# Edge counts summed two tiles ahead of their mask, and source rows requested before the next residual tile

## What is computed

```
xn = layernorm(x)
attn = numerator / max(denominator, 1e-6)                 # first mixer, 8 heads
x_mid = x + attn @ proj_w.T + proj_b + gat(xn, src, dst)
# gat, for each of 4 heads: h = xn @ W
e = leaky_relu(as_[src] + ad_[dst], 0.2)
m = segment_max(e, dst); e = exp(e - m[dst])
alpha = e / segment_sum(e, dst)[dst]
out = segment_sum(h[src] * alpha, dst)
```

## Time and profile before

| | value |
|---|---|
| median of 3 runs | 2633.81 us |
| range of the runs | 2632.14 to 2635.1 us |
| the profiled execution, its device time | 2630.19 us |
| its span in the trace | 2628.4 us |
| TensorE busy | 2555.2 us, 97% of the span |
| VectorE busy | 1587.2 us, 60% |
| ScalarE busy | 769.6 us, 29% |
| GpSimd busy | 347.7 us, 13% |
| mean DMA rate | 61 GB/s |
| VectorE count sums, L1580 | 10 of 1.45 us |
| VectorE masked maxima, L1613 | 100 of 1.46 us in the program, 40 in this stage |

### The profile page before, as it was taken

The page is one execution under the profiler, slowest core; times in us unless marked ns, Lnnn a source line. Parts: engine busy times, 40 slices in busy tenths (PEclk is TensorE's granted clock), DMA queues, the critical chain, the costliest instruction groups (busy, mean ns, idle before and its releaser), DMA issues.

```text
span 2628.4 us, 26650 instructions
## 1 busy us (share of the span) xinstructions
PE 2555.2 (97%) x10594; PEld 1813.6 (69%) x10594; DVE 1587.2 (60%) x2708; ACT 769.6 (29%) x1291; POOL 347.7 (13%) x197
## 2 busy tenths in 40 slices
PE   7999999999999997999999999999999999999999
PEld 4667667558965996777777775565755786556676
DVE  4456471779948996987888998254342561341322
ACT  1043342006732863222222221430002331332000
POOL 0888888000000000000000000000000000000000
PEclk9999999999999998999999999999999999999999
DMA  9232313543020406000120003200450100213201
GB/s 257 26 44 14 50 2 50 143 145 123 20 80 20 116 1 215 1 0 1 72 102 0 24 24 115 70 1 1 115 164 18 37 1 1 63 37 126 87 24 59
DMA packets 139168, 160.74 MB, mean 61 GB/s; under 512 B 96618, under 2 KB 108484, under 8 KB 137516
## 3 DMA queue, kind: packets, MB, share of 16 engines
q1 hardware_dynamic: 68323, 158.60, 19.4%
q0 software_dynamic: 70720, 0.43, 2.8%
HBM read 122.75 MB, written 35.87 MB: 60 GB/s over the span
## 4 chain that ended last, share of the span: by engine, by line
PE 51%; DVE 7%; ACT 2%; issue 1%; DMA 0%; SPq 0%; DVEq 0%; ACTq 0%
PE psum L521 51%; DVE arena L1863 2%; DVE arena L1865 1%; DVE arena L1864 1%; PE psum L532 0%; DVE arena L1856 0%; ACT arena L1126 0%; ACT arena L1131 0%; ACT arena L1015 0%; DVE arena L1519 0%; DVE arena L1929 0%; DVE arena L1361 0%; DVE arena L1862 0%; DVE arena L1855 0%; DVE arena L1888 0%
## 5 line engine op out<-in xcount | busy, mean ns | idle before, releaser
L521 PE MATMUL psum<-arena 128*125 128x384 f32 (+12 forms) x9762 | 2454.4, 413 | 34.8 <-DMA arena<-in_ffn_w 7.1
L521 PEld LDWEIGHTS psum<-arena 128*125 128x125 f32 (+3 forms) x9762 | 1719.8, 188 | 745.5 <-issue 136.7
L2278 POOL DMA_INDIRECT count_matrix<-arena x170 | 343.0, 2018 | 121.1 <-DVE arena L1458 59.7
L1863 DVE RECIPROCAL arena<-arena 128x500 f32<-128x500 f32 x60 | 196.7, 3278 | 2.1
L1613 DVE CUSTOM_DVE_ANT_0 arena<-arena 125x1250 bf16<-125x1250 bf16 (+1 forms) x100 | 139.2, 1458 | 12.9 <-DMA arena<-source_rows 8.3
L2288 POOL MEMSET arena<- 125x60 f32 x1 | 0.2, 208 | 1039.4 <-PE psum L521 1039.4
L1697 DVE TENSOR_TENSOR arena<-arena 125x1250 f32<-125x1250 f32 x80 | 116.3, 1453 | 13.7 <-ACT arena L1108 13.6
L1105 ACT ACTIVATE arena<-arena 125x1250 f32<-125x1250 f32 x80 | 106.9, 1336 | 56.7 <-PE psum L521 56.5
L1700 DVE SCALAR_TENSOR_TENSOR arena<-arena 125x1250 f32<-125x1250 f32 x80 | 116.9, 1461 | 2.8
L1015 ACT ACTIVATE arena<-psum 128x250 f32<-128x250 f32 (+1 forms) x102 | 40.6, 494 | 231.4 <-PE psum L532 230.9
L1248 ACT ACTIVATE arena<-psum,arena 128x250 f32<-128x250 f32 x120 | 49.3, 465 | 198.6 <-PE psum L521 198.6
(11 more groups left out here) (226 smaller groups left out, 1435.0 us busy)
## 6 DMA issues: line engine op xcount, KB each, us to landing
arena<-in_ffn_w SPq DMA_DIRECT2D x3, 4608.0 KB, 14.9
residual<-arena SPq DMA_DIRECT2D x30, 336.0 KB
arena<-residual SPq DMA_DIRECT2D x30, 336.0 KB
arena<-target_rows SPq DMA_DIRECT2D x12, 610.4 KB
arena<-in_gat_w SPq DMA_DIRECT2D x3, 2304.0 KB, 10.5
arena<-residual SPq DMA_DIRECT2D x10, 672.0 KB
residual<-arena SPq DMA_DIRECT2D x10, 672.0 KB
count_matrix<-arena SPq DMA_DIRECT2D x2, 3125.0 KB, 26.9
```

The source lines that it names most:

```text
L521: return pe.matmul(o, lhsT, rhs, start=start, stop=stop, skip_group_check=share)
L1863: now(dve.reciprocal(t_, t_))
L2278: pool.indirect_dma_start(counts[k], bass.IndirectOffsetOnAxis(ap=IDX_I[0:T, c:c + 1].bitcast(U32), axis=0), COUNT_I[0:T, c:c + 1], None, ...
```

## The change

Three things are altered.

1. DVE sums the counts of tile j + 2 behind the mask of tile j, where it summed those of tile j + 1. To begin, it sums tiles 0 and 1 ahead of the first projection. The number of sums stays ten.
2. SP asks for the counts of tile 5 at t = 1 and no longer at t = 2. The other tiles' counts are asked for where they were.
3. SP issues source rows 0 and 1, with the wait for the last mask ahead of them, behind the store of tile 4 and ahead of the wait for that store and the load of tile 6. They were issued behind the load of tile 6. Source row 2 stays where it was.

```diff
-COUNTS_BESIDE = {0: (3,), 1: (4,), 2: (5, 6), 3: (7, 8), 4: (9,)}
+COUNTS_BESIDE = {0: (3,), 1: (4, 5), 2: (6,), 3: (7, 8), 4: (9,)}
...
-                if j + 1 < NT:
-                    count_sum(j + 1)
+                if j + 2 < NT:
+                    count_sum(j + 2)
...
             count_sum(0)
             source_scores(0)
+            count_sum(1)
...
-                if t == 6:
+                if t == 9:
+                    source_row(0, 2)
+
+            def behind_projection(t):
+                if t == 4:
                     sp.wait_ge(as_saved, 16)
                     sp.wait_ge(v_drained, V_AT[("mask", NT - 1, 2)] + 1)
                     source_row(0, 0)
                     source_row(0, 1)
-                if t == 9:
-                    source_row(0, 2)
-
-            residual(0, x, SLOT_M, res[XMID0], beside_projection, begun=True)
+
+            residual(0, x, SLOT_M, res[XMID0], beside_projection, behind=behind_projection, begun=True)
```

## The result

The changed kernel takes 2625.81 us, the median of 12 runs (2623.5 to 2630.97). The kernel before, in 12 runs of the same sessions, takes 2632.2 us. The ratio of the two is 0.9979 with a 95% interval of 0.997 to 0.9988: 5.5 us faster, between 3.2 and 7.9 (the plain difference of the two medians is 6.4). In a later session the same pair gave 0.9986 (0.9977 to 0.9995), 3.7 us, with medians only 2.0 apart. So the size of the gain is known to two or three microseconds and no better. I had forecast 5.0 us and a time between 2626.7 and 2632.0. The profiled execution has a span of 2624.1 us, 4.3 less than the 2628.4 of before.

A forecast was written before the change was run, and what follows sets the result against it. TensorE was taken as the bound, with VectorE nearly as loaded and the order of work causing PE's stalls. 3.97 - 0.6 + 1.68 = 5.0 us, taken from 2633.81, gave 2628.8 us, range 2626.7 to 2632.0.

The forecast's parts named there:

- the source rows' head start: Before the first attention: rows issued 2.8 us earlier land 2.75 us earlier, and that gain reaches L1697 in full.
- The sum: Whole kernel: 3.97 from the masks, less 0.6 for late counts, plus 1.68 at the attention, 5.0 us gained.
- 3.97 us for the masks, at most: Mask stage: TensorE no longer waits for count sums before tiles 3, 5, 7 and 9, four times 0.99 us.
- Rival D: Mask stage: PE stops as before, on the ring of banks; gain 1.7 us, time 2632.1, chance 0.04.
- 0.6 us given back by late counts: Mask stage: DVE waits 0.5 to 0.9 us each for counts of tiles 7 and 9; PE loses 0.3 to 1.05.
- My room of 0.75: Mask stage's ring of banks: PE doesn't stop as long as DVE loses less than 0.75 us in all.
- 1.68 us at the attention: First attention matmuls: DVE holds PE from 610.92 to 612.60; earlier source rows remove this 1.68 us.
- Rival C: Source rows: their head start is not passed on; gain 3.4 to 3.9 us, time 2629.9 to 2630.4, chance 0.12.
- What is now behind the rows: DMA queue: tile 6's load, put behind the rows, lands at 545.9, just before DVE wants it at 546.6.
- The stores of the mask: Before the attention: stores of CT and NEG move by as much as the maxima; DVE didn't stand at their wait before.
- The masks' ring: Mask stage: a half's last three of four banks wait for the previous half's mask banks; room 0.75 us.

The follow-up runs named there:

- the execution with early counts: The changed kernel profiled once more without edit; ratio to the kernel before 0.9986, median 2627.45 us.
- its second profile: The kernel before, profiled once more without edit; span 2625.5 us, ratio 1.0007.
- two kernels: Changed kernel with each source row written by two DMAs (0.9974), and changed kernel with unsplit rows requested at t = 5 (0.9977), ratios to the kernel before.
- rows-alone kernel: Against the changed kernel, sums and count loads put back as before, only the source rows issued earlier; ratio to the kernel before 0.9996.
- the sums alone: Against the changed kernel, source rows put back as before, sums two ahead and tile 5's earlier count load kept; ratio to the kernel before 0.999, median 2626.13 us.
- the second pair: The kernel before and the changed kernel, each profiled once more without edit; ratios 1.0007 and 0.9986.
- the kernel with the delay: Changed kernel plus two needless VectorE copies ahead of the first attention weights; ratio to the kernel before 0.9983.
- the swapped order: Changed kernel with each half's projection ahead of its mask on TensorE and VectorE; ratio to the kernel before 0.9973, median 2623.54 us.

## Why the prediction was wrong

Two steps failed. One put the time outside the range (the level), the other is in the mechanism (the source rows' head start).

**The range.** What put the time outside was mostly the level. I took the median of three runs, 2633.81, for the level of the kernel before. Its median of 12 is 2632.2, 1.6 lower, and in three later sessions it is 2629.4 to 2630.9. The forecast gain of 5.0 us under 2632.2 gives 2627.2; the time came 1.4 below that, as the plain difference of the medians is 6.4 and not 5.0; the ratio puts the gain at 3.2 to 7.9, so that part is within the noise. I had read "three runs spread over 3 us" and still allowed only 1 us of scatter above and 1.5 below. This is the step that put the time outside: "The median of runs lies 3.6 above that execution; I take the same distance", with 1.5 us of room downward. Three runs don't fix the level so closely.

**The sum** came near the measured gain, 5.0 against 5.5 and 3.7, but partly by luck. It contains 1.68 us at the attention that the runs don't show as a gain, and it leaves out the clock, whose single fall is worth as much. That the total came out is no evidence for its terms.

*3.97 us for the masks, at most:* right. With the counts early the halves are 4.96 us apart throughout, and the four stalls of the earlier trace rows are gone in every kernel that sums two ahead. Rival D, that the ring stops TensorE anyway, is refuted.

*0.6 us given back by late counts:* right in mechanism, too small. The waits were 1.3 to 1.5 and 0.7 to 0.9 us, where I had 0.5 to 0.9 each (tile 9's fits, tile 7's doesn't). The part mis-sized is the landing: SP's steps were as predicted (store waited for 2.74, load of x 0.8), but tile 7's counts, followed in the queue by those of tile 8, took 5.4 us from first issue to VectorE's start (501.99 to 507.39) and not 4.51. Tile 9's, with nothing behind, took 4.8. My room of 0.75 was for an execution in which VectorE waits for its first counts and TensorE doesn't start late. None of the profiles is of that kind: the room is 1.15 without VectorE's wait, which agrees with 0.75, as the wait was to be 0.4 to 0.6, and 1.83 where TensorE was late too. Loss: 1.3 in the execution with early counts, 0.2 in the one whose clock had already put TensorE 1.6 behind.

*1.68 us at the attention:* the step of the mechanism that failed. I read the idle 2.04 us and the wait of 4.28 us from one execution as properties of the kernel. In its second profile the gap over the best is 1.16 - 0.74 = 0.42 us. In both kinds of order the row lands 10.8 us after tile 4's end, by the medians of the table (10.8 to 12.0 with the load ahead, 10.2 to 11.1 with it behind; the 7.9 of two kernels is where tile 5 ends). What the earlier issue gained, 2.8 us, the rows lost on their way. "What lay in front of them in the DMA engines was a load of one tile, and is now a store of one tile, 2.75 us earlier" took the two for equal and looked only in front. The load of tile 6, which I had priced as a victim behind the rows, may have been a competitor. The runs show the 2 us that row 0 takes longer, and leave open whether the load behind it or the store ahead of it made them. The rows-alone kernel shows no gain that could be measured, 1.0 us with an interval of 1.3 slower to 3.4 faster. Rival C had this outcome, with a chance of 0.12.

*What is now behind the rows:* right. The load of tile 6 didn't make VectorE wait in any profile.

*The stores of the mask,* which I had moving with the rest, come 0.41 us late in the first profile of the changed kernel and 0.56 in that of the sums alone. In the first of these 0.41 of the 1.08 us by which the gap exceeds the best is theirs, and not the row's. In the kernel before they caused no wait, as I had read, but they must have been nearly due.

*The clock:* missing from the account. Of the 4.3 us between the first two spans, 0.4 lies ahead of L659 (474.50 against 474.89). The masks gave 3.2, of which the start of the stage took 1.6 back (the idle time before the first masks, and the low clock as far as it lies ahead of the first projection), so that the tenth projection is reached 1.6 us sooner, counted from L659. The gap at the attention gave 0.6 and the clock behind it 1.7. These add up to 0.4 + 1.6 + 0.6 + 1.7 = 4.3. (Between the tenth projection and L705 0.1 is lost, and behind L694 as much is gained.) Each of the two profiles has one fall of the clock in it, at different places, and at 1.7 and 1.6 us they nearly cancel. In the second pair neither has one within this stage, and the spans differ by 3.7 us (2625.5 and 2621.8). Of these 2.9 us lie in the stage (294.4 and 291.4): 2.7 in the masks, 0.35 at the attention's gap, less 0.1 between the two. The other 0.8 lie ahead of it (0.4) and behind it (0.4), where the change does nothing.

**What carried the gain** is then, as far as the runs can tell, the sums: 3.97 less 0.2 to 1.3. The two comparisons of parts agree in sum, 2.6 for the sums and 1.0 for the rows, 3.6 against 3.7 for the whole in the same session, but each with an uncertainty of 2.4 us, so the agreement proves little. The 5.5 of the first comparison lies within the whole's interval too (1.3 to 6.1). What shows the sums' share are the profiles: the four stalls are gone in each of the eleven profiles with the sums ahead, and the masks take 1.4 to 3.9 us less, the more the less late the counts are. How often the clock falls at each place of this stage, and whether the change makes that rarer at the attention, stays open: between L659 and L694 the 14 profiles show five falls, one of them in the kernel with the delay and one at a place that no kernel changed, too few for a rate.

## What to carry to other kernels

Take a wait from one profile as a sample and not as a property, above all where it ends with a DMA: profile the unchanged kernel twice before pricing it, and center the range on the spread of the runs. When a DMA is moved forward in a queue, ask what will be behind it and not only what is in front. And before moving a slow transfer, look at how many engines carry it: splitting 125 partitions into 112 and 13 brought the row earlier, which the reordering was meant to do.

## What the runs showed of the hardware

**The clock can fall at short gaps, and one gap does both.** In this stage the granted clock went from 1.00 (2.4 GHz) to its lower level (1.2 GHz) for some microseconds behind idle times of 1.15, 1.26, 2.04 and 2.56 us, and once behind two of 0.92 and 0.65 us around sixty transposes. Each of these falls cost 1.6 to 1.7 us. Behind 2.09 us in another execution it stayed up, as it did behind the 0.92 and 0.65 us in the other thirteen profiles. The second GAT has a better sample. There TensorE stands idle 1.89 us before a group of 200 matmuls, once in nine of the profiles and twice in five, 19 times in all, and the clock fell behind 11 of them:

```profile
915.71 34.63 PE L521 MATMUL psum<-arena 125*125 125x193 f32 x200 [1.89 <-DVE arena L1671]
```

```profile
913.55 33.64 PE L521 MATMUL psum<-arena 125*125 125x193 f32 x200 [1.89 <-DVE arena L1671]
```

The first line is of the changed kernel, with a mean clock of 0.58 in the 2 us from 916; the second is of the swapped order, where it stays up. The same 200 matmuls take 33.64 us or 34.6 to 34.9. But the next 200 start 35.5 us behind these in both, as VectorE releases them, so that nine of the falls cost nothing; the two that came behind the second such gap put off what follows by 1.0 us. So a gap of one or two microseconds has two prices, its length and, where TensorE is what the end waits for, at times a fall of the clock as dear again. What decides between fall and no fall the runs don't show; it is not the gap's length alone.

**A DMA over 125 partitions is slow.** Row 0, of 0.6 MB, was there 7.1 to 10.2 us after its issue, and two rows with the store behind them took 13.7 to 17.2. In 112 and 13 partitions row 0 took 6.1, and the store behind the rows was waited for 537.83 - 534.34 = 3.5 us instead of 9.9. This agrees with the rule of the Trainium skill that the prediction named (page "DMA: Bandwidth & Descriptors", section "Why a DMA increments its semaphore by 16 and not by 1"): five engines of sixteen for 125 partitions is 31%, and the trace has 20 to 30% between the tile transfers.

**The masks' ring** has the sharpest number: where TensorE starts undisturbed VectorE can be late by 1.15 us in all, the same in five profiles to 0.01 us (a sixth has 1.05), and beyond it TensorE loses one for one.
